# A gated block with cross-attention: channel order and transfers of the stacked score operands

## The chip, the cores and the metric

One core of a Trainium2 chip runs the kernel. The metric is the device time of one execution in microseconds; given are the median of three runs and one execution taken with the profiler.

## What is computed

The input x has 16 batches of 256 tokens with 256 channels, the context 16 batches of 256 tokens with 512 channels. Four steps add to x in turn, each behind a tanh gate: a depooled mix with a linear layer (part A below), three cycles of a small coupling network (part B), cross-attention from the normalised x to the context with 8 heads of 32 channels (part C), and a low-rank feed-forward layer (part D). The change lies in part C:

```
src_trans = ctx @ W_src.T + b_src          # 512 outputs: 256 for keys, 256 for values
tgt_trans = layernorm(x) @ W_tgt.T + b_tgt # 256 outputs: queries
(both times mask)
k, v, q   = 8 heads of 32 channels
scores    = q . k / sqrt(32), masked keys at -inf
attn      = softmax(scores)
x         = x + tanh(g) * (concat(layernorm(x), attn . v) @ W_out.T + b_out)
```

## The kernel before, in words

All engines have one program each, written out by hand, with semaphores between them; there is no planner. Only SP (SyncE) issues transfers, and all go through its one queue in the order of its program. Parts A and B are interleaved in twelve slots (`slot_b`); part C then runs over the 16 batches (`body_c`, `last_c`), part D over 8 groups of two batches. Engines other than SP use hardware loops for the middle batches of part C; SP's part is written out for all 16.

**Loads of part C.** `loads_c` (L426 to L436) lists eleven loads: the raw weights, the bias columns, the mask in three forms, and bias rows. SP issues them, with the seven of part D, in `weights_in` (L481) after batch 10 of part A. TensorE turns the raw weights (`turn_weights`, L1252) in slots 7 to 9 of part B into wsrcT, wtgtT and woutT.

**Keys and queries of a batch.** TensorE computes the keys of batch b+2 (`k_c`, L1374) and the queries of batch b+1 (`q_c`, L1401) while batch b is in its softmax. The result is transposed: 128 partitions are output channels, in two groups g of four heads each; head j of a group lies in partitions 32j to 32j+31, and the free dimension is the 256 tokens. VectorE adds the bias and masks (`biased`, L1898) into c_kT and c_qT.

**Parts.** The scores are computed in the fp32r format, with each operand split into a high and a low part. POOL (GpSimd) makes the keys' high and low part (`split_k`, L677 and L679), ScalarE the queries' high part (`high_q`, L938) and POOL their low part (`split_q`, L684). All four are in one tile, c_parts, with 128 partitions, for one batch at a time: the split of the next batch waits until the stacks of the batch before it have landed (semaphore c_stack_in).

**Stacks.** One product a head then covers three terms at once: the contraction has 97 rows, three strips of 32 (q high, q low, q high against k high, k high, k low) and one row with 1 against the mask. SP fills c_stack, one of two by turns, in `stack_c`: for each strip c and head j one copy (L526) of 32 partitions, queries and keys together, 128 KB; then the mask row (L530). That is 13 transfers a batch (STACK_DMAS). Before them SP waits for both key parts, for the queries' low part, and for the scores of two batches back, which read the same stack. Behind them SP issues the load of the context of batch b+2 (`stream_c`, L516). TensorE's `scores_c` (L1413) waits for all 13.

**Order on TensorE in `body_c`** (a batch b): scores of the first four heads; queries of b+1; values of b+1; transposes of the probabilities of b-1 (L1435); the output of b-1 (L1456); scores of the last four heads; transposes of the context of b+2 (L1366) and its keys (L1374); transposes of the normalised x of b+2 (L1384); the update (L1449). Before batch 0 TensorE prepares batches 0 and 1 and takes the last results of part B back (L1240), interleaved with the last slots of part B.

The names above are those of the rows: b_o, b_t, b_tt belong to part B; c_nmx is the negated maximum of the scores (VectorE, L1914), c_p the probabilities (ScalarE, L956), n_mv and n_tmp the statistics for part D.

Of the kernel before, what the change touches and what calls it, by code (L numbers as in the profile page):

```python
# [18 lines left out]
F32 = mybir.dt.float32  # L19
# [7 lines left out]
P = 128  # L27
B, S, D, DC = 16, 256, 256, 512
TILES = B * S // P
TS = S // P  # L30
DK = D // P
FK = DC // P
# [4 lines left out]
HEADS, HD = 8, 32  # L37
QH = 4
# [23 lines left out]
Q_LO, Q_HI, K_HI, K_LO = range(PARTS)  # L62
GCOL = 8
MASK_ROW = 3 * HD
STACK_DMAS = 3 * QH + 1
LEAD = 2
HEAD = 6
KB = 1024
# [48 lines left out]
def need(eng, sem, count):  # L117

    if isinstance(count, int) and count <= 0:
        return  # L120
    eng.wait_ge(sem, count)


def need_alone(eng, sem, count, passed):


    if isinstance(count, int):
        return need(eng, sem, count)
    eng.wait_ge(sem, count)
    eng.sem_inc(passed, 1)  # L130
# [33 lines left out]
def beyond(b, n):  # L164
    return isinstance(b, int) and b >= n
# [14 lines left out]
def build(nc, x, ctx_in, lens, mask, g_xattn, g_ffn, w_in, b_in, g_res, g_init,  # L180
# [7 lines left out]
    with ExitStack() as whole:  # L188
        def sb(name, shape, dt=F32, stack=whole):
            return stack.enter_context(nc.sbuf_tensor(name, shape, dt))  # L190

        def sem(name):
            return whole.enter_context(nc.semaphore(name))
# [26 lines left out]
        bk_col = sb("bk_col", [P, DK])  # L220
        bq_col = sb("bq_col", [P, DK])
# [90 lines left out]
        with ExitStack() as st:  # L312
            sb("raw_first", [P, 74 * KB // 4], F32, st)
            wsrc_raw = sb("wsrc_raw", [P, FK, DC], F32, st)
            wtgt_raw = sb("wtgt_raw", [P, DK, D], F32, st)
            wout_raw = sb("wout_raw", [P, DK, 2 * D], F32, st)
        with ExitStack() as st:
# [6 lines left out]
            c_stack = [None, sb("c_stack1", [MASK_ROW + 1, 2, QH, DK, S], F32R, st)]  # L324
# [9 lines left out]
            c_parts = sb("c_parts", [P, PARTS, DK, S], F32R, st)  # L334
# [5 lines left out]
        with ExitStack() as st:  # L340
# [24 lines left out]
        s_passed = sem("waits_passed")  # L365
# [26 lines left out]
        c_k_split, c_qhi_ok, c_qlo_ok, c_stack_in = (sem("c_" + n) for n in (  # L392
            "k_parts_ready", "q_high_ready", "q_low_ready", "stacks_in"))
        c_s_ps, c_mx_ok, c_p_ok, c_inv_ok, c_pn_ok = (sem("c_" + n) for n in (
            "scores_in_psum", "max_ready", "probs_ready", "inverse_sums_ready", "probs_normalised"))
# [15 lines left out]
        def column(v):  # L411
            return v.rearrange("(c p) -> p c", p=P)

        def row_on_all(v):
            return v.partition_broadcast(P)


        loads_a = [
            (gates_row[:, 0:4:2], g_xattn.rearrange("(o c) -> o c", o=1)),
# [3 lines left out]
        ]  # L423
        rows_a = [(ginit_b[:], row_on_all(g_init[0:D])), (bin_b[:], row_on_all(b_in))]
        loads_c = [
            (wsrc_raw[:], w_src.rearrange("(c p) f -> p c f", p=P)),  # L426
            (wtgt_raw[:], w_tgt.rearrange("(c p) f -> p c f", p=P)),
            (wout_raw[:], w_out.rearrange("(c p) f -> p c f", p=P)),
            (bk_col[:], column(b_src[0:D])), (bq_col[:], column(b_tgt)),
            (mask_b[:], mask.partition_broadcast(P)),  # L430
            (mask_col[:], mask.rearrange("b (k p) -> p b k", p=P)), (neg_row[:], mask),
            (bout_b[:], row_on_all(b_out)), (b2_b[:], row_on_all(b2)), (bv_b[:], row_on_all(b_src[D:2 * D])),
# [43 lines left out]
        def _(sp):  # L476
# [37 lines left out]
            def stream_c(b, s):  # L514
                need(sp, c_ctxT_ps, 2 * (b - 1))
                sp.dma_start(c_ctx[s][:], ctx_dram[b]).then_inc(c_ctx_in[s], 16)  # L516

            def stack_c(b, s):
                if isinstance(b, int) and b == 1:
                    sp.wait_ge(b_ok[3], 2 * PAIRS)  # L520
                need_alone(sp, c_k_split, 2 * b + 2, s_passed)
                need_alone(sp, c_qlo_ok, b + 1, s_passed)
                need_alone(sp, c_s_ps, 2 * TS * (b - 1), s_passed)
                for c, (first, step) in enumerate(((Q_HI, K_HI - Q_HI), (Q_LO, K_HI - Q_LO), (Q_HI, K_LO - Q_HI))):
                    for j in range(QH):
                        sp.dma_start(  # L526
                            c_stack[s][c * HD:(c + 1) * HD, :, j, :, :].rearrange("p a g t -> p a (g t)").bitcast(F32),
                            c_parts[j * HD:(j + 1) * HD, first:first + step + 1:step, :, :]
                            .rearrange("p a g t -> p a (g t)").bitcast(F32)).then_inc(c_stack_in, 16)
                sp.dma_start(  # L530
                    c_stack[s][MASK_ROW:MASK_ROW + 1, 1, :, :, :].rearrange("p j g t -> p (j g) t").bitcast(F32),
                    neg_row[b:b + 1, :].unsqueeze(1).to_broadcast([1, QH * DK, S])).then_inc(c_stack_in, 16)

            def body_stack(b, s):
                stack_c(b, s)
                if not beyond(b + 2, B):
                    stream_c(b + 2, s)

            stream_c(0, 0)
            stream_c(1, 1)  # L540
            sp.wait_ge(s_neg, 1)
            for b in range(B):
                body_stack(b, b % 2)

            def store(n, s):
                need(sp, d_y_ok, 2 * (n + 1))
# [16 lines left out]
        def _(pool):  # L563
# [110 lines left out]
            def split_k(b):  # L674
                need_alone(pool, c_k_ok, b + 1, s_passed)
                need_alone(pool, c_stack_in, 16 * STACK_DMAS * b, s_passed)
                nc.gpsimd.tensor_copy(c_parts[:, K_HI, :, :], c_kT[:]).then_inc(c_k_split, 1)  # L677
# [55 lines left out]
        def _(act):  # L733
# [201 lines left out]
            def high_q(b):  # L935
                need(act, c_q_ok, b + 1)
                need(act, c_stack_in, 16 * STACK_DMAS * b)
                nc.scalar.copy(c_parts[:, Q_HI, :, :], c_qT[:]).then_inc(c_qhi_ok, 1)  # L938
# [138 lines left out]
        def _(pe):  # L1077
# [327 lines left out]
            def scores_c(b, s, hg):  # L1405
                need(pe, c_stack_in, 16 * STACK_DMAS * (b + 1))
                if isinstance(b, int) and b < 2:
# [693 lines left out]
```

## Time and profile before

| what | us |
|---|---|
| median of three runs | 712.64 |
| lowest and highest of them | 712.11 and 713.82 |
| the profiled execution | 712.77 |
| its span, from first to last instruction | 710.7 |
| TensorE busy in it | 681.4 |
| VectorE busy | 512.4 |
| ScalarE busy | 418.1 |
| POOL busy | 209.7 |

The profiled execution has 2.07 us more than its span. Times in rows are microseconds from the start of the span. PE is TensorE's products, PEld its weight loads (they overlap), DVE VectorE, ACT ScalarE, POOL GpSimd, SPq the queue of SP. An L with a number is a line of the kernel.

### The profile page before, as it was taken

To read this page: it belongs to the slowest core of one execution; us is meant where nothing else is said; L and a number is where in the kernel's file an instruction comes from. 1 tells how busy PE (TensorE), PEld (TensorE's weight loads), DVE (VectorE), ACT (ScalarE), POOL (GpSimd) and SP (SyncE) were. 2 spreads that over 40 slices of the span, in tenths; PEclk is the share of its full clock that TensorE was granted. 3 is DMA by queue.
4 is the path that set the end of the run, shared out by engine and by line. 5 is a ranking of instruction groups with operands and counts; after the bars stand their busy time and mean duration, and the time that the engine had idled before them with its cause. 6 is when DMAs were issued, how large, how long until landed. Compare 5 with 4: busy or idle time off the path is not lost.

```text
span 710.7 us, 12199 instructions
## 1 busy us (share of the span) xinstructions
PE 681.4 (96%) x3877; PEld 478.4 (67%) x3877; DVE 512.4 (72%) x976; ACT 418.1 (59%) x1128; POOL 209.7 (30%) x285
## 2 busy tenths in 40 slices
PE   5799899999999999999999999999999998999997
PEld 3565555554544358788888888888888886756654
DVE  7864757776775458898889888888888888734422
ACT  7656665535555535656756657657667657645453
POOL 6564424200110033233343432332323330052110
PEclk9999999999999999999999999999999999999999
DMA  8721108401000004444323444333444323001012
GB/s 260 237 101 60 59 31 253 79 6 56 1 0 1 0 1 119 120 120 119 76 79 88 119 120 100 87 76 94 119 119 92 85 47 74 3 0 60 30 60 89
DMA packets 44970, 57.54 MB, mean 81 GB/s; under 512 B 13018, under 2 KB 23420, under 8 KB 44796
## 3 DMA queue, kind: packets, MB, share of 16 engines
q1 hardware_dynamic: 44924, 56.96, 29.8%
q8 instruction: 24, 0.39, 0.2%
q14 instruction: 22, 0.18, 0.1%
HBM read 27.46 MB, written 4.19 MB: 45 GB/s over the span
## 4 chain that ended last, share of the span: by engine, by line
PE 79%; ACT 7%; DVE 6%; issue 3%; POOL 2%; SPq 1%; DMA 1%; DVEq 0%; ACTq 0%; POOLq 0%
PE bank L1160 11%; PE bank L1456 8%; PE bank L1374 7%; PE bank L1435 7%; PE bank L1172 5%; PE bank L1392 5%; ACT c_p L956 5%; PE bank L1413 4%; PE bank L1449 4%; PE bank L1592 4%; PE bank L1136 3%; PE bank L1582 2%; PE bank L1140 2%; PE bank L1583 2%; DVE c_nmx L1914 2%
## 5 line engine op out<-in xcount | busy, mean ns | idle before, releaser
L956 ACT ACTIVATE c_p<-bank,c_nmx 128x256 f32<-128x256 f32 x256 | 117.3, 487 | 26.2 <-DVE c_nmx L1914 26.2
L1160 PE MATMUL bank<-b_o,cw 128*128 128x512 f32 x192 | 90.8, 603 | 0.2 <-ACT b_o L808 0.2
L1927 DVE TENSOR_TENSOR c_p<-c_p,c_inv 128x1024 f32<-128x1024 f32 x64 | 90.1, 1408 | 1.1
L1914 DVE TENSOR_REDUCE c_nmx<-bank 128x4 f32<-128x1024 f32 x64 | 75.4, 1218 | 13.4 <-PE bank L1413 13.4
L1435 PE MATMUL bank<-ident,c_p 128*128 128x128 f32 x512 | 65.4, 276 | 2.2 <-ACT c_p L956 1.6
L1435 PEld LDWEIGHTS bank<-ident,c_p 128*128 128x128 f32 x512 | 58.2, 142 | 10.0 <-issue 4.5
L784 ACT ACTIVATE b_h<-bank,cb 128x512 f32<-128x512 f32 x48 | 32.8, 686 | 51.2 <-PE bank L1160 51.2
L1059 ACT ACTIVATE d_h<-bank,b_col 128x512 f32<-128x512 f32 x64 | 39.6, 686 | 39.6 <-PE bank L1583 39.6
L1374 PE MATMUL bank<-c_ctxT,wsrcT 128*128 128x256 f32 x256 | 61.4, 385 | 0.7 <-ACT c_ctxT L932 0.7
L1160 PEld LDWEIGHTS bank<-b_o,cw 128*128 128x128 f32 x192 | 34.1, 190 | 41.3 <-issue 39.2
L1934 DVE COPY c_pT<-bank 128x512 f32<-128x512 f32 x64 | 43.7, 685 | 18.0 <-PE bank L1435 18.0
L1392 PE MATMUL bank<-wsrcT,c_ctxT 128*128 128x256 f32 x240 | 56.7, 379 | 0.0
L956 ACT ACTIVATION_READ_ACCUMULATOR c_p<-bank,c_nmx 128x1 f32 x256 | 56.3, 220 | 0.0
L684 POOL TENSOR_TENSOR c_parts<-c_qT,c_parts 128x512 fp32r<-128x512 f32 x16 | 20.9, 1303 | 118.4 <-ACT c_parts L938 118.4
L1374 PEld LDWEIGHTS bank<-c_ctxT,wsrcT 128*128 128x128 f32 x256 | 47.9, 192 | 7.0 <-ACT c_ctxT L932 0.9
L1392 PEld LDWEIGHTS bank<-wsrcT,c_ctxT 128*128 128x128 f32 x240 | 45.5, 190 | 6.2
L966 ACT COPY c_pT<-bank 128x512 f32<-128x512 f32 x64 | 38.0, 598 | 10.1 <-PE bank L1435 10.0
L1772 DVE TENSOR_SCALAR b_tt<-b_tt,k_tt,b_kb 128x256 f32<-128x256 f32 x48 | 19.7, 452 | 33.4 <-ACT b_tt L800 33.4
L1172 PE MATMUL bank<-b_h,cw 128*128 128x512 f32 x96 | 43.7, 593 | 0.0
L1413 PEld LDWEIGHTS bank<-c_stack 97*128 97x128 f32 x256 | 32.4, 189 | 13.0 <-issue 12.5
L971 ACT COPY c_upT<-bank 128x256 f32<-128x256 f32 x32 | 12.0, 375 | 46.9 <-PE bank L1449 46.9
L1413 PE MATMUL bank<-c_stack 97*128 97x256 f32 x256 | 38.9, 294 | 0.6 <-DMA c_stack<-neg_row 0.3
(194 smaller groups left out, 1384.4 us busy)
## 6 DMA issues: line engine op xcount, KB each, us to landing
c_stack<-c_parts SPq DMA_DIRECT2D x192, 128.0 KB
a_ctx<-in_ctx SPq DMA_DIRECT2D x16, 512.0 KB, 3.8
c_ctx<-in_ctx SPq DMA_DIRECT2D x16, 512.0 KB, 3.5
out_x<-x_sb SPq DMA_DIRECT2D x7, 512.0 KB, 2.9
x_sb<-in_x SPq DMA_DIRECT2D x3, 1024.0 KB, 10.2
mask_b<-in_mask_BxS_fk SPq DMA_DIRECT2D x1, 2048.0 KB, 12.1
x_sb<-in_x SPq DMA_DIRECT2D x2, 512.0 KB, 5.9
wsrc_raw<-in_L_xattn_W_src SPq DMA_DIRECT2D x1, 1024.0 KB, 6.8
```

The costliest lines, as they stand in the source:

```text
L956: op = nc.scalar.activation(c_p[hg][:, tc, j, :], scores(tc)[:, j, :], ACT.Exp, bias=c_nmx[hg][:, tc, j:j + 1], accum_out=c_sum[hg][:, tc, ...
L1059: op = nc.scalar.activation(d_h[j % 2][:, e, :], bank[2 * (j % 2) + e][:], ACT.Gelu_apprx_tanh, bias=b1_col[:, 2 * j + e:2 * j + e + 1])
L1160: op = mm(bank[2 * u + h][:], cw1[:, c, h * P:(h + 1) * P], b_o[n % LANES][:, c, :], start=c == 0, stop=c == DK - 1)
L1172: op = mm(bank[4 + u][:], cw2[:, c, :], b_h1[u][:, c, :], start=i == 0, stop=i == DK - 1)
L1374: op = mm(bank[dst][:, m * S:(m + 1) * S], wsrcT[:, f, m * P:(m + 1) * P], c_ctxT[s][:, f, :], start=f == 0, stop=f == FK - 1)
L1392: op = mm(bank[4][:, k * D:(k + 1) * D], c_ctxT[s][:, f, k * P:(k + 1) * P], wsrcT[:, f, D:2 * D], start=f == 0, stop=f == FK - 1)
L1413: op = mm(scores(tc)[:, j, :], c_stack[s][:, 0, j, hg, tc * P:(tc + 1) * P], c_stack[s][:, 1, j, hg, :], start=True, stop=True)
L1435: op = nc.tensor.transpose(bank[turned_bank(n, j)][:, q * S + tc * P:q * S + (tc + 1) * P], c_p[hg][:, tc, j, q * P:(q + 1) * P], ident[:])
L1456: return mm(bank[7][:, k * D:(k + 1) * D], src[:, k * P:(k + 1) * P], woutT[:, f, :], start=f == 0, stop=f == 2 * DK - 1)
L1914: v.tensor_reduce(c_nmx[hg][:, tc, :], scores(tc), AXIS.X, ALU.max, negate=True)\
L1927: v.tensor_tensor(pr, pr, c_inv[hg][:, :, js].unsqueeze(3).to_broadcast([P, TS, 2, S]), ALU.mult)\
L1934: v.tensor_copy(c_pT[hg][:, j, :], bank[turned_bank(n, j)][:]).then_inc(c_pT_dve, 1)
```

## The change

The key and query channels within each group of four heads are stored in the order (channel of the head, head), so that the four heads lie side by side: partition 4d + j in place of 32j + d. This is done by the loads of the weights' rows and of the biases; the values' rows keep their order. One copy then takes all 128 partitions of one part into one strip of the stack: six copies of 256 KB, three for the keys' side and three for the queries'. SP issues the keys' side, with the mask row, as soon as the keys' parts are ready, and the queries' side behind its own wait.

```diff
--- before.py
+++ after.py
@@ -62,7 +62,7 @@
 Q_LO, Q_HI, K_HI, K_LO = range(PARTS)
 GCOL = 8
 MASK_ROW = 3 * HD
-STACK_DMAS = 3 * QH + 1
+STACK_DMAS = 7
 LEAD = 2
 HEAD = 6
 KB = 1024
@@ -414,6 +414,9 @@
         def row_on_all(v):
             return v.partition_broadcast(P)
 
+        def heads_mixed(v):
+            return v.rearrange("(j d) o -> d j o", d=HD)
+
 
         loads_a = [
             (gates_row[:, 0:4:2], g_xattn.rearrange("(o c) -> o c", o=1)),
@@ -423,10 +426,14 @@
         ]
         rows_a = [(ginit_b[:], row_on_all(g_init[0:D])), (bin_b[:], row_on_all(b_in))]
         loads_c = [
-            (wsrc_raw[:], w_src.rearrange("(c p) f -> p c f", p=P)),
-            (wtgt_raw[:], w_tgt.rearrange("(c p) f -> p c f", p=P)),
+            *((wsrc_raw[:, c, :], heads_mixed(w_src[c * P:(c + 1) * P])) for c in range(DK)),
+            (wsrc_raw[:, DK:FK, :], w_src[D:2 * D].rearrange("(c p) f -> p c f", p=P)),
+            *((wtgt_raw[:, c, :], heads_mixed(w_tgt[c * P:(c + 1) * P])) for c in range(DK)),
             (wout_raw[:], w_out.rearrange("(c p) f -> p c f", p=P)),
-            (bk_col[:], column(b_src[0:D])), (bq_col[:], column(b_tgt)),
+            *((bk_col[:, c:c + 1], heads_mixed(b_src[c * P:(c + 1) * P].rearrange("(p o) -> p o", o=1)))
+              for c in range(DK)),
+            *((bq_col[:, c:c + 1], heads_mixed(b_tgt[c * P:(c + 1) * P].rearrange("(p o) -> p o", o=1)))
+              for c in range(DK)),
             (mask_b[:], mask.partition_broadcast(P)),
             (mask_col[:], mask.rearrange("b (k p) -> p b k", p=P)), (neg_row[:], mask),
             (bout_b[:], row_on_all(b_out)), (b2_b[:], row_on_all(b2)), (bv_b[:], row_on_all(b_src[D:2 * D])),
@@ -515,32 +522,34 @@
                 need(sp, c_ctxT_ps, 2 * (b - 1))
                 sp.dma_start(c_ctx[s][:], ctx_dram[b]).then_inc(c_ctx_in[s], 16)
 
-            def stack_c(b, s):
-                if isinstance(b, int) and b == 1:
+            def sides_c(b, s, side, firsts):
+                for c, part in enumerate(firsts):
+                    sp.dma_start(
+                        c_stack[s][c * HD:(c + 1) * HD, side, :, :, :].rearrange("p j g t -> p j (g t)").bitcast(F32),
+                        c_parts[:, part, :, :].rearrange("p g t -> p (g t)").bitcast(F32)).then_inc(c_stack_in, 16)
+
+            def keys_c(b, s):
+                if b == 1:
                     sp.wait_ge(b_ok[3], 2 * PAIRS)
-                need_alone(sp, c_k_split, 2 * b + 2, s_passed)
-                need_alone(sp, c_qlo_ok, b + 1, s_passed)
-                need_alone(sp, c_s_ps, 2 * TS * (b - 1), s_passed)
-                for c, (first, step) in enumerate(((Q_HI, K_HI - Q_HI), (Q_LO, K_HI - Q_LO), (Q_HI, K_LO - Q_HI))):
-                    for j in range(QH):
-                        sp.dma_start(
-                            c_stack[s][c * HD:(c + 1) * HD, :, j, :, :].rearrange("p a g t -> p a (g t)").bitcast(F32),
-                            c_parts[j * HD:(j + 1) * HD, first:first + step + 1:step, :, :]
-                            .rearrange("p a g t -> p a (g t)").bitcast(F32)).then_inc(c_stack_in, 16)
+                need(sp, c_k_split, 2 * b + 2)
+                need(sp, c_s_ps, 2 * TS * (b - 1))
+                sides_c(b, s, 1, (K_HI, K_HI, K_LO))
                 sp.dma_start(
                     c_stack[s][MASK_ROW:MASK_ROW + 1, 1, :, :, :].rearrange("p j g t -> p (j g) t").bitcast(F32),
                     neg_row[b:b + 1, :].unsqueeze(1).to_broadcast([1, QH * DK, S])).then_inc(c_stack_in, 16)
 
-            def body_stack(b, s):
-                stack_c(b, s)
-                if not beyond(b + 2, B):
-                    stream_c(b + 2, s)
+            def queries_c(b, s):
+                need(sp, c_qlo_ok, b + 1)
+                sides_c(b, s, 0, (Q_HI, Q_LO, Q_HI))
 
             stream_c(0, 0)
             stream_c(1, 1)
             sp.wait_ge(s_neg, 1)
             for b in range(B):
-                body_stack(b, b % 2)
+                keys_c(b, b % 2)
+                queries_c(b, b % 2)
+                if b + 2 < B:
+                    stream_c(b + 2, b % 2)
 
             def store(n, s):
                 need(sp, d_y_ok, 2 * (n + 1))
```

## Rows read from the trace of the kernel before

**Rows 1.** Waits, whole run: engine, line, releaser: us in total, times, longest

```profile
PE bank L1413 <- DMA c_stack<-neg_row: 0.3, 1, 0.3
...
PE bank L1366 <- DVE c_vb L1906: 0.9, 1, 0.9
PE bank L1374 <- ACT c_ctxT L932: 0.7, 1, 0.7
...
POOL c_parts L677 <- DVE c_kT L1898: 70.6, 15, 10.2
```

**Rows 2.** Steady batch: length, busy PE, PEld, DVE, ACT, POOL, clock, DMA share, GB/s

```profile
338.50:359.90 21.40, 21.38 (x153) 17.96 (x149) 19.18 (x35) 13.88 (x45) 7.74 (x10) 1.00 0.40 100
```

**Rows 3.** The chain of waits at batch 0: start, us, what

```profile
264.83 1.28 POOL c_parts L679
...
266.20 0.73 SPq L526
...
274.04 2.03 DMA c_stack<-neg_row
```

**Rows 4.** TensorE in order of time before batch 0: start, us, line, tiles, count, idle before

```profile
271.83 3.72 PE L1374 MATMUL bank<-c_ctxT,wsrcT 128*128 128x256 f32 x16
275.38 0.60 PE L1384 MATMUL bank<-ident,c_xn 128*128 128x128 f32 x4
276.31 1.18 PE L1413 MATMUL bank<-c_stack 97*128 97x256 f32 x8 [0.33 <-DMA c_stack<-neg_row]
```

**Rows 5.** Busy time by stretch while stack 0 moves (columns of rows 2)

```profile
266.00:267.50 1.50, 1.50 (x9) 0.89 (x6) 1.50 (x4) 0.89 (x2) 1.34 (x2) 1.00 0.00 0
...
268.50:275.00 6.50, 6.50 (x39) 5.79 (x39) 6.39 (x12) 1.88 (x4) 0.00 (x0) 1.00 0.88 205
```

**Rows 6.** SP's queue in order of time, stack of batch 1

```profile
284.08 9.28 SPq L526 DMA_DIRECT2D c_stack<-c_parts  x12
...
286.68 2.19 SPq L526 DMA_DIRECT2D c_stack<-c_parts  x1
...
293.40 0.72 SPq L530 DMA_DIRECT2D c_stack<-neg_row  x1
```

**Rows 7.** POOL, TensorE and SP in order of time, batch 1 and a steady batch

```profile
277.48 1.27 POOL L679 TENSOR_TENSOR c_parts<-c_kT,c_parts 128x512 fp32r<-128x512 f32 x1
...
282.72 1.27 POOL L684 TENSOR_TENSOR c_parts<-c_qT,c_parts 128x512 fp32r<-128x512 f32 x1 [2.12 <-ACT c_parts L938]
...
295.65 1.21 PE L1413 MATMUL bank<-c_stack 97*128 97x256 f32 x8
...
346.33 1.27 POOL L684 TENSOR_TENSOR c_parts<-c_qT,c_parts 128x512 fp32r<-128x512 f32 x1 [3.85 <-ACT c_parts L938]
...
347.66 7.68 SPq L526 DMA_DIRECT2D c_stack<-c_parts  x12
355.38 0.70 SPq L530 DMA_DIRECT2D c_stack<-neg_row  x1
...
359.89 1.22 PE L1413 MATMUL bank<-c_stack 97*128 97x256 f32 x8
```

**Rows 8.** SP and TensorE in order of time, stack and scores of the last batch

```profile
591.37 0.71 SPq L530 DMA_DIRECT2D c_stack<-neg_row  x1
...
594.39 1.22 PE L1413 MATMUL bank<-c_stack 97*128 97x256 f32 x8
```

**Rows 9.** SP and TensorE in order of time, loads of weights and first use

```profile
111.89 1.04 SPq L481 DMA_DIRECT2D bq_col<-in_L_xattn_b_tgt  x1
...
129.71 3.06 SPq L481 DMA_DIRECT2D v_sb<-in_L_ffn_V  x2
...
199.54 1.04 PE L1252 MATMUL bank<-ident,wsrc_raw 128*128 128x128 f32 x8
```

**Rows 10.** ScalarE in order of time, first exponential of batch 0

```profile
278.32 0.47 ACT L956 ACTIVATE c_p<-bank,c_nmx 128x256 f32<-128x256 f32 x1 [0.41 <-DVE c_nmx L1914]
```

**Rows 11.** Busy time by stretch after batch 0's idle times (columns of rows 2)

```profile
288.00:291.00 3.00, 3.00 (x11) 2.43 (x10) 1.72 (x3) 3.00 (x14) 0.00 (x0) 0.50 0.46 107
```

## The prediction

> **What bounds the kernel now.** The page names TensorE as the busiest engine, so I read its waits first, then the seam where the attention part (part C) begins, then one steady batch and the last one. The list of waits says what ended TensorE's idle time: in all its rows only one wait, of 0.3 us, ended with a stack transfer; the two larger ones of part C, 0.9 and 0.7 us, ended with VectorE's and ScalarE's work [rows 1]. In a steady batch TensorE works 21.38 of 21.40 us at a granted clock of 1.00 (its 2.4 GHz level), while VectorE works 19.18 us and the DMA engines have a share of 0.40 [rows 2]. So part C runs at the pace of TensorE, and a transfer matters only where it lands later than TensorE's earlier work ends.
>
> The place where it does is batch 0. SP waits for the low part of the keys (POOL, 264.83 + 1.28 us), issues twelve copies from 266.20 to 274.04 us, 0.65 us each, and then the mask row, which lands 2.03 us later, at 276.07 [rows 3]. TensorE ends the preparation of batch 1 at 275.38 + 0.60 = 275.98 us and starts the scores at 276.31, after 0.33 us of idle time [rows 4]. The chain of waits passes through SP there, which looks like eight microseconds of transfer on the path; but TensorE has other work beside all of it up to 275.98 us, without idle time [rows 4]. From this seam I take the whole gain, 0.33 us and not the length of the chain.
>
> **The change, part by part.**
>
> *Copies of the stacks.* Twelve copies of 128 KB go and six of 256 KB come: the same 1.57 MB a batch, and in both forms one contiguous run is 2 KB. Issues fall from 13 to 7. At 0.65 us each that is 4.6 us in place of 8.5 us [rows 3]. No row shows a copy from 128 partitions into 32, so its data rate has to be bounded. The fast end: issue was the limit, and the engines, at a share of 0.88 with 205 GB/s [rows 5], could give 205 / 0.88 = 233 GB/s; 1.57 MB is then 6.7 us. The middle: 205 GB/s stays, 7.7 us. The slow end: batch 1, whose copies began at 284.08 and whose mask row, issued at 293.40, landed some 2.03 us later, near 295.4 [rows 3, 6]: 1.57 MB in 11.3 us, 139 GB/s. I take 205 GB/s: it is the rate of the same bytes in runs of the same length, steady over 6.5 us. Data began 1.3 us after the first issue (nothing moves before 267.5) [rows 5]. So the last byte arrives at 267.5 + 7.7 = 275.2. From there to the landing it takes nothing at the least and at the most what the same sum leaves of before, 276.07 - 275.2 = 0.9 us; I take the middle, 0.4, thus 275.6 us, ahead of 275.98. The fast end gives 274.6; 0.9 us in place of 0.4 gives 276.1, the first rival below.
>
> A rule of the Trainium skill speaks against the change here: "SBUF — State Buffer", section "Door 1: The DMA port swizzle (why [64,N] ≈ [32,N])", says that the rate of a transfer depends on how many of 16 ports its partitions reach, that 32 partitions reach eight, and gives 27.2 GB/s for each. By it the writes, still into strips of 32 partitions, stay below about 218 GB/s though the reads now span 128, so that wider copies buy no rate; the sum would have 7.2 us of data and the same end.
>
> *Order and waits.* SP now waits for the keys' parts and for the scores of two batches back, issues three copies and the mask row, then waits for the low part of the queries and issues three more. In batch 0 POOL made the queries' part before the keys' parts, so both waits end at 266.12 us and the order brings nothing. In batch 1 the keys' parts are ready at 277.48 + 1.27 = 278.75 us and the queries at 282.72 + 1.27 = 283.99 [rows 7]; the keys' side lands before the queries are there, and three copies remain: half the data at the slow 139 GB/s is 5.7 us, plus 1.3 and 0.4, landing near 291.4, for scores that start at 295.65 [rows 7]. Before, the landing at about 295.4 left only 0.2 us there; it becomes over 4. In a steady batch SP issues the mask row at 355.38, which lands near 357.4, for scores at 359.89 [rows 7]. With the queries ready at 346.33 + 1.27 = 347.60 and three copies to go, the landing moves to about 353 and the slack of 2.5 us to about 7: worth nothing, costs nothing. The last batch is the same: mask row at 591.37, landing near 593.4, scores at 594.39 [rows 8].
> Behind SP's new waits stand the queries' copies and the load of the context of two batches on. Six issues less stand ahead of that load, so it goes out some 3.9 us earlier than now. Behind the landing of all seven transfers stand POOL's split of the next keys and ScalarE's high part of the queries; but POOL's 70.6 us of waiting before its key split all end with VectorE's keys, none with a transfer [rows 1], so an earlier landing frees nobody.
>
> *Weights and biases in mixed order.* Eleven loads become sixteen: five more issues on SP, at up to 1.04 us each some 5 us at most, with the same bytes, in runs of 1 or 2 KB for the weights and 4 bytes for the biases. SP's last load is issued by 129.71 + 3.06 = 132.8 us; the first turn of a weight on TensorE is at 199.54 us [rows 9]. The cover is TensorE's 67 us of part B; without it they would cost their 5 us. Cost: nothing. TensorE, ScalarE and VectorE run the same instructions on the same shapes everywhere, at no cost.
>
> *Sum.* The profiled execution took 712.77 us: its span of 710.7 and 2.07 around it. TensorE's wait of 0.33 us goes. What is late next is the softmax of batch 0: the first exponential waited 0.41 us for VectorE's maxima, after ScalarE had been free [rows 10], and the maxima need these scores; so all of it can follow 0.33 us earlier. 712.77 - 0.33 = 712.44. The median of the runs lies 0.13 us under the profiled execution, so I forecast **712.3 us**.
>
> **The rivals.** I take 0.3% (2.1 us) as about what a measurement of this kernel can tell from no change: faster begins at 710.5, slower at 714.8.
>
> *No gain at all.* If the data rate and not the issue set the end, or if the wide copies are a little slower than 205 GB/s, or take the 0.9 us to land, batch 0 lands at 276.1 as before and the time stays 712.6. For it: 205 GB/s is just 128 KB per 0.64 us, so the rows of batch 0 can't tell rate from issue. Against it: in a steady batch too the twelve issues took an even 7.68 us [rows 7]; a queue held back by data would be less even. 0.25.
>
> *Slower: batch 0 waits for slow copies.* Each copy now reads 128 partitions and writes 32, a form that no row shows. At the 139 GB/s of batch 1 its data ends at 267.5 + 11.3 = 278.8 us and lands at 279.2: 279.2 - 275.98 = 3.2 us of waiting in place of 0.33, so 712.6 + 2.9 = 715.5 us. It decides from 2.1 us of added wait on, a landing at 278.4, a rate under 1.57 MB / (278.4 - 0.4 - 267.5) = 150 GB/s. Only batch 0 pays; all others have the slack above. Against it: what stretched batch 1 was one issue of 2.19 us in the midst of normal ones [rows 6], not the rate of the copies. 0.07.
>
> *The clock.* After TensorE's idle times of 0.9 and 0.7 us [rows 1] at the end of batch 0, the granted clock was 0.50 (1.2 GHz) from 288 to 291 us [rows 11], with TensorE busy throughout: 3 us of work that takes 1.5 us at 2.4 GHz. These idle times wait for VectorE and ScalarE and not for a stack, so they stay; but all of it comes 0.33 us earlier, and the fall may turn on that. If it doesn't come: 712.3 - 1.5 = 710.8. If another of its size comes elsewhere: 713.8. 0.06 and 0.04.
>
> *The change does not do what it says.* The order of the channels could force runs shorter than 2 KB and so more of them. The patterns say otherwise: the last dimension of both sides stays 512 numbers. It would end as the slower rival does, and is in its chance.
>
> **How the numbers follow.** Forecast 0.58, no gain 0.25, slow copies 0.07, clock kept 0.06, clock lost twice 0.04. The first two hold 0.83, at 712.3 and 712.6; the runs before lay 0.5 us below and 1.2 us above their median, which makes 711.8 to 713.8. To take in part of the kept clock I go down to 711.4. Faster (under 710.5) takes half of the kept clock's chance with its run-to-run spread: 0.04. Slower takes most of the slow copies and the top of the clock lost twice: 0.07. The rest, 0.89, is the same.
>
> **What would show it.** In the profile after: no idle time before the scores of batch 0 that ends with a transfer, these scores at 275.98; the last of seven issues at about 270.1 us; in each steady batch two groups on SP, four issues near its start and three after the queries; still 21.40 us a batch. If the landing in batch 0 stays near 276.1, the rate set it and not the issue. The prediction is wrong if the period of the batches moves, if TensorE waits over 1 us for a stack anywhere, or if a time under 711 comes without a change of the clock.

## The result, and the profile after

The changed kernel is slower: a median of 719.80 us over four executions (717.20 to 720.99) against 712.61 us for the kernel before (four executions). The medians lie 7.2 us apart, 1.0%; the means lie 6.7 us apart, and the ratio follows them: 1.0093 with a 95% interval of 1.0063 to 1.0124. The profiled execution was the lowest of the four, 717.20 us, with a span of 715.4 us. One of the four executions of e5_gaps below fell in a slow state (995.34 us at a granted clock of 0.66) and is left out of its figures.

The number of issues came out as intended, and the order too. SP's queue in order of time, in batches 0 and 1:

```profile
264.27 1.98 SPq L527 DMA_DIRECT2D c_stack<-c_parts  x3
266.29 0.75 SPq L537 DMA_DIRECT2D c_stack<-neg_row  x1
267.08 1.89 SPq L527 DMA_DIRECT2D c_stack<-c_parts  x3
269.01 0.61 SPq L523 DMA_DIRECT2D c_ctx<-in_ctx  x1
281.33 1.85 SPq L527 DMA_DIRECT2D c_stack<-c_parts  x3
```

Seven issues take 4.7 us (264.27 to 268.97), where thirteen took 8.5 [rows 3]. But TensorE, in order of time:

```profile
273.46 0.60 PE L1393 MATMUL bank<-ident,c_xn 128*128 128x128 f32 x4
279.40 2.04 PE L1422 MATMUL bank<-c_stack 97*128 97x256 f32 x8 [5.34 <-DMA c_stack<-c_parts]
281.24 3.62 PE L1410 MATMUL bank<-c_xnTq,wtgtT 128*128 128x256 f32 x8
284.65 2.02 PE L1401 MATMUL bank<-wsrcT,c_ctxT 128*128 128x256 f32 x8
```

It was ready at 274.06 us and waited 5.34 us for the stack, where it had waited 0.33 [rows 4]. The copies were all issued by then; it is their data that took the time. Busy time by stretch (the columns of rows 2; the last two are the DMA share and GB/s):

```profile
264.00:265.50 1.50, 1.50 (x8) 0.84 (x5) 1.50 (x4) 0.82 (x2) 1.43 (x2) 1.00 0.00 0
...
268.00:270.00 2.00, 2.00 (x19) 1.83 (x17) 2.00 (x5) 1.23 (x3) 0.00 (x0) 1.00 1.07 122
270.00:272.00 2.00, 2.00 (x11) 1.77 (x11) 1.93 (x4) 0.65 (x2) 0.00 (x0) 1.00 1.08 123
272.00:274.00 2.00, 2.00 (x12) 1.59 (x10) 2.00 (x5) 0.00 (x0) 0.00 (x0) 1.00 1.11 127
274.00:276.00 2.00, 0.06 (x1) 0.00 (x0) 0.80 (x3) 1.87 (x2) 0.00 (x0) 1.00 1.04 119
```

122 GB/s at a DMA share of 1.07, where the copies before moved 205 GB/s at 0.88 [rows 5]. A share of 1 is not a rate: the engines were held longer for the same bytes. During the wait the granted clock fell:

```profile
274.00:279.40 5.40, 0.06 (x1) 0.03 (x1) 0.80 (x3) 1.87 (x2) 0.12 (x1) 0.88 1.03 147
279.40:284.00 4.60, 4.60 (x15) 4.06 (x16) 2.36 (x2) 2.11 (x9) 3.57 (x3) 0.50 0.43 99
284.00:285.00 1.00, 1.00 (x5) 0.79 (x4) 0.10 (x1) 1.00 (x6) 0.00 (x0) 0.55 1.10 127
...
321.70:343.10 21.40, 21.38 (x152) 17.98 (x148) 19.19 (x35) 13.88 (x45) 7.75 (x10) 1.00 0.62 99
```

From 279.4 us on TensorE worked for some 5.5 us at 0.50 (1.2 GHz): all of the 4.6 us up to 284.0, and nine tenths of the microsecond after them. The last line is a steady batch: 21.38 us busy of 21.40, as before [rows 2]; only the DMA share rose, from 0.40 to 0.62 for the same bytes.

The books of the profiled pair need the later starts of the same work, first before, then after:

```profile
280.79 1.04 PE L1240 MATMUL bank<-ident,b_o 128*128 128x128 f32 x8
287.14 3.01 PE L1374 MATMUL bank<-c_ctxT,wsrcT 128*128 128x256 f32 x8 [0.69 <-ACT c_ctxT L932]
292.39 1.89 PE L1374 MATMUL bank<-c_ctxT,wsrcT 128*128 128x256 f32 x8
```

```profile
286.50 1.04 PE L1249 MATMUL bank<-ident,b_o 128*128 128x128 f32 x8
292.42 1.99 PE L1383 MATMUL bank<-c_ctxT,wsrcT 128*128 128x256 f32 x8 [0.69 <-ACT c_ctxT L941]
296.17 1.06 PE L1444 MATMUL bank<-ident,c_p 128*128 128x128 f32 x8 [0.76 <-ACT c_p L965]
297.07 1.89 PE L1383 MATMUL bank<-c_ctxT,wsrcT 128*128 128x256 f32 x8
```

| term | us |
|---|---|
| TensorE ready for the first scores at 274.06 in place of 275.98 | -1.9 |
| wait for stack 0, 5.34 in place of 0.33 | +5.0 |
| slow clock behind it: 279.40 to 286.50 took 7.1, 276.31 to 280.79 took 4.5 | +2.6 |
| shorter wait for c_vb, 0.45 in place of 0.88 | -0.4 |
| the slow stretch of before [rows 11] did not occur, less a new wait | -0.6 |

The sum is 4.7 us, the whole difference of the spans (715.4 and 710.7). The slow stretch had lasted over 3 us, but its absence gave only 0.6 us (292.42 to 297.07 against 287.14 to 292.39), because TensorE then caught up with ScalarE and waited 0.76 us for the probabilities.

The first term is luck of this execution, as far as the runs show. In the profiled executions of the other five kernels with the mixed loads TensorE was ready between 274.4 and 275.5 us, and in four with the loads of before (before, e6_forms, e9_held, e10_forms2) between 274.0 and 276.0; the two ranges overlap. The other three executions of the changed kernel took 719.6 to 721.0 us.

### The profile page after: what moved, and what is told of

Its sections match the earlier page's. It is cut to its first block, busy times and chain, and to the rows that moved or that the text cites. A ratio compares the mean times of both kernels' runs of the same rounds, so it can differ in the third digit from the quotient of the medians.

```text
span 715.4 us, 12108 instructions
## 1 busy us (share of the span) xinstructions
PE 680.8 (95%) x3877; PEld 478.0 (67%) x3877; DVE 512.2 (72%) x976; ACT 418.2 (58%) x1128; POOL 208.7 (29%) x285
## 4 chain that ended last, share of the span: by engine, by line
PE 78%; ACT 8%; DVE 6%; issue 3%; POOL 2%; DMA 2%; SPq 1%; DVEq 0%; ACTq 0%; POOLq 0%
PE bank L1169 11%; PE bank L1465 8%; PE bank L1444 7%; PE bank L1383 7%; ACT c_p L965 5%; PE bank L1181 5%; PE bank L1401 5%; PE bank L1422 4%; PE bank L1458 4%; PE bank L1601 4%; PE bank L1145 3%; PE bank L1591 2%; PE bank L1149 2%; PE bank L1592 2%; DVE c_nmx L1923 2%
## 5 line engine op out<-in xcount | busy, mean ns | idle before, releaser
L1444 PE MATMUL bank<-ident,c_p 128*128 128x128 f32 x512 | 64.9, 274 | 2.9 <-ACT c_p L965 2.3
L1444 PEld LDWEIGHTS bank<-ident,c_p 128*128 128x128 f32 x512 | 57.3, 141 | 11.0 <-issue 5.6
```

Source lines behind the costliest of these rows:

```text
L1444: op = nc.tensor.transpose(bank[turned_bank(n, j)][:, q * S + tc * P:q * S + (tc + 1) * P], c_p[hg][:, tc, j, q * P:(q + 1) * P], ident[:])
```

## The experiments

**Where in the kernel is the loss?** Three kernels ask this. In `e4_first12` batch 0 alone goes back to twelve copies, one for each head and strip (in the mixed order these read every fourth partition); the others stay as changed.

```diff
             for b in range(B):
-                keys_c(b, b % 2)
-                queries_c(b, b % 2)
+                if b == 0:
+                    strided_c(b, b % 2)
+                else:
+                    keys_c(b, b % 2)
+                    queries_c(b, b % 2)
...
+                for c, (first, step) in enumerate(...):
+                    for j in range(QH):
+                        sp.dma_start(c_stack[s][c * HD:(c + 1) * HD, :, j, :, :]...,
+                                     c_parts[j:P:QH, first:first + step + 1:step, :, :]...)
```

The counts of landed copies that the other engines wait for follow; that part is left out here.

> The changed kernel with the stack of batch 0 alone filled by the twelve copies of one head each; batches 1 to 15 keep six wide copies and early keys. Theory 1 (only batch 0 pays): 712 to 713.5 us, TensorE's wait for a stack under 0.5 us, the granted clock at 0.50 in one stretch of 3 us at most after it. Rival (the slow copies cost something in every batch, through contention or through the context load behind them): 715 us or more, with a period of the batches over 21.5 us or new waits of 0.2 us and more.

Measured: 715.44 us, ratio to before 1.0049 (1.0031 to 1.0068). The wait was 3.22 us, not under 0.5: these copies are slow too, at some 150 GB/s.

```profile
278.01 1.22 PE L1446 MATMUL bank<-c_stack 97*128 97x256 f32 x8 [3.22 <-DMA c_stack<-neg_row]
279.03 3.57 PE L1434 MATMUL bank<-c_xnTq,wtgtT 128*128 128x256 f32 x8
```

So both numbers that I gave missed, and the time is even past the rival's 715 us; but neither sign of the rival is there. A batch takes 21.40 us still, and no other wait is for a stack. In the profiled pair there are 2.9 us more of waiting and 1.7 us for the clock, which fell 1 us after the wait and stayed at 0.50 for some 3.3 us; TensorE was ready 1.2 us earlier, and 0.4 and 0.6 us came off as in the changed kernel. That makes 2.4 of the 2.5 us between the spans, all of it in batch 0.

In `e7_queries_first` all copies stay wide; in batch 0 alone the queries' side, which POOL makes first, is issued first.

```diff
-                keys_c(b, b % 2)
+                if b > 0:
+                    keys_c(b, b % 2)
                 queries_c(b, b % 2)
+                if b == 0:
+                    keys_c(b, b % 2)
```

> The changed kernel, but in batch 0 alone the queries' three copies go ahead of the keys' side, since POOL has their parts 3.9 us earlier. Theory 1 (the loss is the late landing in batch 0 and the clock that follows): the first data moves from some 261.5 us on, 1.57 MB at 122 GB/s end at 274.5 and land at 274.9, TensorE is ready at 274.0: a wait of about 0.9 us in place of 5.3, no long stretch of slow clock right after it, and a time of 712.5 to 714 us. Rival (wide copies cost in all batches): 715 us or more.

Measured: 712.69 us over ten executions, ratio 1.0008 (0.9996 to 1.0020). TensorE in order of time:

```profile
274.71 0.60 PE L1396 MATMUL bank<-ident,c_xn 128*128 128x128 f32 x4
276.70 1.19 PE L1425 MATMUL bank<-c_stack 97*128 97x256 f32 x8 [1.40 <-DMA c_stack<-neg_row]
277.73 1.89 PE L1413 MATMUL bank<-c_xnTq,wtgtT 128*128 128x256 f32 x8
```

The wait is 1.40 us, more than the 0.9 I had estimated, and the product after it takes 1.89 us, the time at 2.4 GHz, where it took 3.62. Fifteen wide stacks, the early keys and the mixed loads together cost nothing that the medians of ten and nineteen executions show, and nothing near 7 us.

One reservation stands against "nothing". Nine of the ten executions had a mean granted clock of 0.997 or 0.998, and spans of 710.1 to 711.4 us. The kernel of before had that clock in seven of nineteen, with spans of 708.7 to 709.2; in the other twelve, at 0.993 to 0.995, they were 710.0 to 712.6. At a like clock e7_queries_first is thus some 2 us longer. Its wait, 1.1 us longer than before's, is about half of that; what the other half is (the slow copies of later batches, the loads, or something else) no run shows.

`e9_held` is the opposite: the kernel of before, with fast copies everywhere, where only the last four copies and the mask row of batch 0 are held back.

```diff
                     for j in range(QH):
+                        if b == 0 and c * QH + j == 3 * QH - 4:
+                            sp.wait_ge(c_xnT_ps, 2)
                         sp.dma_start(
```

> The kernel of before with its fast copies, but the last four copies and the mask row of batch 0 are held back until TensorE has ended its work ahead of the scores (275.98 us), so that the stack lands some 5.3 us after that (five issues of 0.65 us and 2.03 us), as late as in the changed kernel; no other batch is touched. Theory 1 (a late landing in batch 0 and the slow clock after it are the whole loss): 718.5 to 720.5 us, with 1.2 GHz for some 6 us after the wait. Rival (part of the loss comes from the slow copies of the other batches): 717.5 us or less, and the rest up to 719.8 is theirs.

Measured: 718.52 us, ratio 1.0093 (1.0074 to 1.0111), the ratio of the change itself. The wait came to 4.86 us, and the clock fell as in the changed kernel, for a shorter time:

```profile
274.99 0.60 PE L1386 MATMUL bank<-ident,c_xn 128*128 128x128 f32 x4
280.44 2.05 PE L1415 MATMUL bank<-c_stack 97*128 97x256 f32 x8 [4.86 <-DMA c_stack<-neg_row]
282.29 2.62 PE L1403 MATMUL bank<-c_xnTq,wtgtT 128*128 128x256 f32 x8
```

The same kernel, busy time and clock in the stretch behind the wait:

```profile
280.40:284.00 3.60, 3.56 (x13) 3.30 (x14) 2.33 (x2) 1.07 (x5) 3.46 (x3) 0.53 0.33 124
```

A late landing in batch 0 and the clock behind it, put into the old kernel by hand, give 6.4 us over the 712.13 us of before in that comparison. The wait was 0.5 us shorter than the change's, and the slow clock behind it cost 1.5 us (280.44 to 286.46 for the 4.5 us of before) where it had cost 2.6, because it lasted some 3.3 us and not 5.5 (nor the 6 expected); against this, the later slow stretch of before came here too. The interval is 1.3 us wide on either side, so a loss of about 1 us in the other batches is not excluded by this run.

**Did the early keys matter?** `e1_late` keeps the wide copies and undoes the order.

```diff
                 need(sp, c_k_split, 2 * b + 2)
+                need(sp, c_qlo_ok, b + 1)
                 need(sp, c_s_ps, 2 * TS * (b - 1))
```

> The changed kernel with its early keys undone: SP waits for the queries' low part too before it issues any of the seven transfers; the form of the copies stays. Theory 1 (the wide copies themselves move only some 122 GB/s, so stack 0 lands 5 us too late for TensorE and everything else is hidden): nothing changes against the changed kernel, TensorE waits 5 to 5.5 us for stack 0 and a time of 717 to 721 us, since both waits end together in batch 0; in a steady batch the landing moves from about 6 us ahead of the scores to 0 or 1 us ahead (1.57 MB at 122 GB/s is 12.9 us, started 12.2 us before the scores), so a small wait per batch is possible, up to 2 us each, 740 us at the worst. Theory 2 (the early issue costs, because keys' copies stand in the queue when context loads or queries should go): faster than the changed kernel, 712 to 714 us.

Measured: 791.02 us, ratio 1.1098 (1.1036 to 1.1160), far beyond both. The list of waits (engine, line, releaser: us in total, times, longest us):

```profile
POOL c_parts L687 <- DMA c_stack<-c_parts: 104.0, 15, 14.3
...
PE bank L1423 <- DMA c_stack<-c_parts: 49.0, 16, 5.4
```

And busy time in one stretch of the same kernel, late in part C:

```profile
426.40:450.80 24.40, 23.34 (x136) 20.06 (x140) 16.04 (x24) 13.12 (x44) 9.82 (x9) 0.86 0.49 69
```

POOL waits because it may split the next keys only after the stack has landed. TensorE waited in all sixteen batches, some 2.9 us each after the first. In the four batches after batch 0 (304 to 402 us) the clock still stayed at 1.00, with waits of 2.5 to 2.9 us; then it was 0.93 over one stretch of 24.4 us and 0.86 over each of the next four. TensorE was busy for 711.9 us in place of 680.8 with the same instructions. My bound counted the waits, with 2 us each, and forgot the clock. So the change has two halves of opposite sign: the wide copies alone would cost 11%, and the early keys take nearly all of that back. Their order in the queue costs nothing (the second theory falls).

**What makes the copies slow?** `e2_strided` undoes the width and keeps the mixed order, with twelve copies as in e4_first12 in all batches and the old waits.

```diff
-                keys_c(b, b % 2)
-                queries_c(b, b % 2)
+                strided_c(b, b % 2)
```

> Channel order as in the changed kernel, but the stacks filled by twelve copies again, each from the 32 partitions of one head (every fourth one), queries and keys together, with all waits first. Theory 1 in the form that the width of a copy (128 partitions read, strips of 8 KB written) is slow: the rate is back at 205 GB/s, stack 0 lands at 276 on the clock of the profile of before, TensorE waits under 0.5 us, the time is 712 to 713.5 us. In the form that the mixed order of partitions is slow to read whatever the copy: DMA share near 1 at some 122 GB/s, wait of 5 us, 717 to 721 us. Rival (the mixed order of the loads costs something in the earlier parts): 1.57 MB moves at 205 GB/s but the time stays over 715 us.

Measured: 729.16 us, ratio 1.0247 (1.0226 to 1.0268). The rate during stack 0 is between the two:

```profile
268.00:270.00 2.00, 2.00 (x18) 1.88 (x17) 2.00 (x5) 0.92 (x2) 0.00 (x0) 1.00 1.11 158
270.00:272.00 2.00, 2.00 (x12) 1.73 (x11) 1.93 (x5) 0.96 (x3) 0.00 (x0) 1.00 1.04 145
272.00:274.00 2.00, 2.00 (x12) 1.72 (x12) 2.00 (x4) 0.00 (x0) 0.00 (x0) 1.00 1.10 151
```

Neither answer I had offered fits: the width is not the whole of it, since the strided copies of 32 partitions, 128 KB each as before, give some 150 and not 205 GB/s. With all waits first they delay every batch (14.2 us of waits for stacks in sixteen batches).

`e5_gaps` takes the other suspect, the 8 KB that each partition of the stack receives in one piece: with queries and keys of a head side by side these are four runs of 2 KB with gaps. The mask row takes two transfers then (left out below).

```diff
-sb("c_stack1", [MASK_ROW + 1, 2, QH, DK, S], F32R, st)
+sb("c_stack1", [MASK_ROW + 1, QH, 2, DK, S], F32R, st)
...
-c_stack[s][c * HD:(c + 1) * HD, side, :, :, :]
+c_stack[s][c * HD:(c + 1) * HD, :, side, :, :]
```

> The changed kernel with another layout of the stack: queries and keys of one head side by side, so that one partition receives four runs of 2 KB with gaps of 2 KB between them, and not 8 KB in one piece; the mask row takes two transfers instead of one. Reads, number and size of the copies as in the changed kernel. Theory W (four runs of one partition in one piece, or packets of more than 2 KB, slow the writes): the rate goes back to about 205 GB/s, TensorE's wait under 0.5 us, 712 to 713.5 us. Theory R (what is slow is the reading of 128 neighbouring partitions, or engines that meet at one port): 122 GB/s as before, a wait of 5 to 6 us (one issue more), 717 to 721 us.

Measured: 719.02 us (three executions), ratio 1.0098 (1.0077 to 1.0120). TensorE waited 5.4 us, the rate was 118 to 128 GB/s. The runs are not the cause.

So two kernels measured forms of copies by themselves, in the kernel of before: after the stack of each of ten batches, four extra copies of 256 KB, one form for a batch, each waited for before the next is issued. They read the turned weights and write a part of the memory that is free then.

```diff
+            def probe(b):
+                sp.wait_ge(c_ctx_in[b % 2], 16 * ((b + 2) // 2 + 1))
+                for i in range(4):
+                    sp.dma_start(*forms[b - 3]).then_inc(s_probe, 16)
+                    sp.wait_ge(s_probe, 64 * (b - 3) + 16 * (i + 1))
```

> The kernel of before, with four extra copies of 256 KB after the stack of each of ten batches (3 to 12), one form for each batch, each copy waited for before the next; they read the turned weights and write into a part of the memory that is free then, so the result stays; the time has no meaning here, only the spacing of the issues and the GB/s of the DMA engines by form. The forms in order: (1) 128 partitions to the same 128, (2) 128 to 32, the form of the change, (3) 32 to 128, (4) 32 to the same 32 in runs of 8 KB, (5) the same in runs of 2000 bytes, (6) partitions 64 to 95 to 0 to 31, (7) every fourth partition to 0 to 31, (8) 0 to 31 to every fourth, (9) every fourth to the same, (10) 128 to 64 to 95. Theory A (engines meet at the partitions that a narrow side has, so a narrow write or a narrow read gives the limit): 1 fastest, 2, 3, 4 and 10 alike near 200 GB/s at most. Theory B (what counts is that each engine reads and writes the partitions of the same place; a copy whose two sides are laid out differently is slow): 1, 4, 5 and 9 fast (1 and 9 over 250, 4 and 5 some 200 GB/s), 2, 3, 10 near 122, 7 and 8 near 148 GB/s. Theory C (runs or size: 8 KB against 2 KB): 4 and 5 differ, and 2 is like 5.

> The kernel of before with extra copies of 256 KB as in e6_forms, other forms: (1) partitions 0 to 31 to the same, (2) 32 to 63 to 0 to 31, (3) 16 to 47 to 0 to 31, (4) 4 to 35 to 0 to 31, (5) 0 to 63 to the same, (6) 64 to 127 to 0 to 63, (7) every second of 128 to 0 to 63, (8) 0 to 63 to 0 to 31, (9) 128 to 0 to 63, (10) 128 to 0 to 31. The spacing of the issues counts; e6_forms gave 3.0 us for 32 to the same 32 and 4.0 us for 128 to 32. Theory B1 (each engine should read and write the same place; any shift of one side is slow): 3 and 4 take 3.5 us or more, 2 and 6 stay at 3.0 because they were as fast as their like in e6_forms (64 partitions apart). Theory B2 (a shift is harmless; slow is a copy whose two sides divide the partitions differently, so that engines meet at few partitions on one side): 2, 3, 4 and 6 all stay near 3.0, 7, 8 and 9 lie between 3.0 and 4.0 us, 10 at 4.0 us.

Each was profiled in one execution. The spacing from the second issue to the third, in us (the spacings within a form agree within 0.1 us, but for the first of the very first form and one of 3.72 where partitions 4 to 35 were read):

| from | to | e6_forms | e10_forms2 |
|---|---|---|---|
| 128 | the same 128 | 2.31 | |
| every fourth of 128 | the same | 2.37 | |
| 32 | the same 32, run of 8 KB | 3.05 | 2.99 |
| 32 | the same 32, runs of 2000 bytes | 3.02 | |
| 64 to 95 | 0 to 31 | 2.90 | |
| 32 to 63 | 0 to 31 | | 2.91 |
| 16 to 47 | 0 to 31 | | 2.93 |
| 4 to 35 | 0 to 31 | | 2.95 (last) |
| 64 | the same 64 | | 3.01 |
| 64 to 127 | 0 to 63 | | 2.90 |
| 0 to 31 | every fourth | 3.44 | |
| 32 | 128 | 3.54 | |
| every fourth | 0 to 31 | 3.85 | |
| every second | 0 to 63 | | 3.90 |
| 64 | 32 | | 3.91 |
| 128 | 64 | | 4.02 |
| 128 | 32 (the form of the change) | 4.00 | 4.00 |
| 128 | 64 to 95 | 4.00 | |

Three classes stand out. A copy to the same partitions, or to ones shifted by 4, 16, 32 or 64, takes 2.9 to 3.1 us where its sides are 32 or 64 neighbours, and 2.3 to 2.4 where they spread over all 128. A copy whose sides divide the partitions differently takes 3.4 to 4.0, and halving the number (128 to 64, 64 to 32) is as slow as quartering it: the second theory of e10_forms2 holds, with its "between 3.0 and 4.0" at the top of that range (3.90, 3.91, 4.02). The first theory of each (a narrow side, or any shift) falls, and so does the third of e6_forms, as runs of 8 KB and of 2000 bytes take the same (3.05 and 3.02).

How a slow copy goes is seen in quarters of a microsecond. First 128 partitions to the same, in e6_forms, the columns as before:

```profile
343.93:344.18 0.25, 0.25 (x5) 0.25 (x4) 0.22 (x3) 0.11 (x1) 0.00 (x0) 1.00 0.44 172
344.18:344.43 0.25, 0.25 (x5) 0.25 (x4) 0.25 (x1) 0.06 (x1) 0.00 (x0) 1.00 1.02 393
344.43:344.68 0.25, 0.25 (x5) 0.25 (x3) 0.25 (x1) 0.25 (x1) 0.00 (x0) 1.00 1.01 393
344.68:344.93 0.25, 0.25 (x3) 0.23 (x3) 0.25 (x1) 0.25 (x2) 0.00 (x0) 1.00 0.25 90
```

Then 128 to 32, the same 256 KB, in the same kernel:

```profile
364.83:365.08 0.25, 0.25 (x3) 0.02 (x1) 0.25 (x1) 0.25 (x3) 0.00 (x0) 1.00 0.89 352
365.08:365.33 0.25, 0.22 (x3) 0.24 (x3) 0.25 (x2) 0.25 (x1) 0.00 (x0) 1.00 1.15 377
365.33:365.58 0.25, 0.25 (x4) 0.25 (x3) 0.22 (x3) 0.12 (x1) 0.00 (x0) 1.00 1.28 139
365.58:365.83 0.25, 0.25 (x5) 0.25 (x4) 0.25 (x1) 0.05 (x1) 0.00 (x0) 1.00 1.04 106
365.83:366.08 0.25, 0.25 (x5) 0.25 (x4) 0.25 (x1) 0.25 (x1) 0.00 (x0) 1.00 0.55 66
```

It starts as fast as the other and falls to some 110 GB/s after half a microsecond, with every engine still held. That looks like data piling up ahead of a few places of the side written; which engine writes where is not in the trace, so this reading is an inference. It would also say why a single copy does not show the low rate from its start and a queue of them does.

**Was the small gain there at all?** In `e8_ones_later` the kernel of before starts its copies of batch 0 earlier, as POOL's fill of the row of ones (1.80 us) moves behind the key split.

```diff
             split_q(0)
-            ones_c(0, c_qlo_ok, 1)
             split_k(0)
+            ones_c(0, c_k_split, 2)
```

> The kernel of before, but POOL fills the row of ones of stack 0 (1.80 us) after it has split the keys of batch 0, and not ahead of it. The copies then start 1.8 us earlier. If the 0.33 us of TensorE's wait in batch 0 was all that the stacks cost before, the wait goes and the time falls by 0.3 us to 712.1, which can't be told from no change: 711.5 to 712.5 us.

Measured: median 711.55 us over ten executions, but the ratio is 1.0001 (0.9990 to 1.0011). TensorE's wait for the stack is gone from the list and a new one stands ahead of it:

```profile
269.79 1.04 PE L1366 MATMUL bank<-ident,c_ctx 128*128 128x128 f32 x8
271.59 1.09 PE L1240 MATMUL bank<-ident,b_o 128*128 128x128 f32 x8 [0.77 <-DVE b_o L1779]
272.52 3.62 PE L1374 MATMUL bank<-c_ctxT,wsrcT 128*128 128x256 f32 x16
...
276.33 1.20 PE L1413 MATMUL bank<-c_stack 97*128 97x256 f32 x8
```

The scores of batch 0 begin without a wait, at 276.33 us, the 276.31 of before. But the edit moved more than the copies. VectorE before, then VectorE and POOL in e8_ones_later:

```profile
267.33 0.74 DVE L1772 TENSOR_SCALAR b_tt<-b_tt,k_tt,b_kb 128x256 f32<-128x256 f32 x2
```

```profile
267.05 1.82 DVE L1772 TENSOR_SCALAR b_tt<-b_tt,k_tt,b_kb 128x256 f32<-128x256 f32 x2
267.13 1.27 POOL L671 TENSOR_TENSOR x_sb<-x_sb,bout_b 128x512 f32<-128x512 f32 x1
```

POOL's addition at L671, which comes after the fill in its program, ran at 266.07 us before and now runs beside two instructions of VectorE's update, which take 1.82 us in place of 0.74. TensorE, 0.27 us ahead of before at 269.79, then waits 0.77 us for that update. That the one delays the other is my reading of these rows; no run tests it. The copies also start only 0.9 us earlier (265.29 against 266.20), not 1.8, because POOL waits for VectorE's keys first. So this way of taking the wait away is worth nothing that can be measured; whether the 0.33 us could be had without the side effect stays open.

## Why the prediction was wrong, point by point

*What bounds the kernel.* Right: TensorE sets the pace, only batch 0 can wait for a stack, and a steady batch takes 21.40 us still.

*The count of issues.* Right: seven issues in 4.7 us, estimated at 4.6.

*The rate of the wide copy.* This is the step that failed: "I take 205 GB/s: it is the rate of the same bytes in runs of the same length". The rate measured is 122 GB/s. Bytes and run length were the wrong measure of likeness; what counts is whether both sides divide the partitions alike, and no copy in the trace of before did anything else. The slow end of my bounds, 139 GB/s, did not hold it either: it came from a stretch of batch 1 that one issue of 2.19 us had stretched, which says nothing on the rate of any copy. A form that no row shows has no lower bound in rows of another form. With 122 GB/s the same sum gives, on the clock of the profile after, data from 265.5 + 12.9 = 278.4 and a landing near 278.8; TensorE got it by 279.40.

*The rule of the Trainium skill* that I weighed, in "SBUF — State Buffer", section "Door 1: The DMA port swizzle (why [64,N] ≈ [32,N])", spoke against the gain, but not enough: it allows 218 GB/s for writes to 32 partitions, and 122 were measured. Where both sides are alike it agrees with the forms: 64 neighbours took 3.01 us as 32 did (2.99 to 3.05), and 32 partitions spread over all 128 took 2.37 us, near the 2.31 of all 128. Counting the partitions of one side was not sufficient: a copy of 32 partitions to the same 32 has the same narrow side and took 3.0 us, the form of the change 4.0.

*The rival "batch 0 waits for slow copies"* was the case that came, with the place I gave and the sign. It was priced at 715.5 us for 139 GB/s and had 0.07. Two of its terms were too small: the wait (3.2 us estimated, 5.34 measured) and the clock, which I had treated as a rival by itself instead of as a part of this one. [Rows 11] showed that 1.6 us of idle time in the same batch was followed by 1.2 GHz; a wait of over 3 us had to be priced with such a stretch as well. 712.6 + 5.0 + 2.6 = 720.2 us, against 719.8 measured.

*Order and waits.* "Worth nothing, costs nothing" was right for fast copies and wrong for these. In the steady batch the queries' copies are issued at 352.29 us:

```profile
345.86 1.86 SPq L527 DMA_DIRECT2D c_stack<-c_parts  x3
...
352.29 1.88 SPq L527 DMA_DIRECT2D c_stack<-c_parts  x3
...
364.55 1.21 PE L1422 MATMUL bank<-c_stack 97*128 97x256 f32 x8
```

Half the data at 122 GB/s is 6.4 us, so I estimate the landing at 352.3 + 1.3 + 6.4 + 0.4 = 360.4 us, 4 us ahead of the scores. With the whole stack behind the queries it would be 366.9, late by more than 2 us: e1_late showed 2.9 us a batch.

*The loads in mixed order* cost nothing that can be told apart: e7_queries_first has them, with the reservation made there. *The gain of 0.33 us* is neither confirmed nor refuted: e8_ones_later removed that wait, but its side effect put another one in its place.

*The clock as a rival.* In the profile after, the slow stretch at 288 us was gone, and that was worth 0.6 us and not the 1.5 of the sum. The prediction had passed over a wait of TensorE in part C that is in the same list: 1.6 us in three waits for ScalarE's probabilities (L1435). It grew to 2.3 us in four (L1444) once the clock was kept. The chance of 0.06 was small too: of the nineteen executions of before that were taken later, seven had a clock of 0.997 or 0.998.

*The chances.* 0.07 for the slow copies was too little for a quantity I had just called unbounded by any row, when its error costs ten times what the forecast gains (2.9 us against 0.33). With 0.3 us to win and all of the landing at risk in batch 0, the side on which an error falls should have set the chances.

## What to carry to other kernels

Fewer transfers are not faster transfers: a copy within the on-chip memory whose two sides divide the partitions differently (128 to 32, every fourth to neighbours) ran at some 120 and 150 GB/s in a queue here, one of 32 partitions to 32 neighbours at 205, so measure the form of a copy by itself before the layout of a kernel is built on it. Before a stage whose operands need a pipeline of transfers, look at its first pass: in fifteen batches the slack hid the slow copies, and only because the keys' side went out early; the first batch, with no slack, paid. And price a TensorE wait with the slow clock that may follow it: here 5.0 us more of waiting brought 2.6 us of slow clock with it.

## What the runs showed of the hardware that I had not expected

A copy of 256 KB from 128 partitions to 64 is as slow as one to 32 (4.02 and 4.00 us, against 2.31 to the same 128), while a shift by 4, 16, 32 or 64 partitions costs nothing (2.9 us each, against 3.0 for the same partitions). A slow copy begins at up to 377 GB/s and falls to 106. The reverse direction, 32 to 128, is less slow, 3.54 us.

In e1_late waits of 2.5 to 2.9 us left the granted clock of TensorE at 1.00 for four batches; later ones, of 2.5 to 4.5 us, went with a clock of 0.86 over a batch, and the busy time rose from 680.8 to 711.9 us. After a single idle time of 1.40 us in e7_queries_first the clock stayed at 1.00 for the next 14 us; after one of 3.22 us in e4_first12 it fell 1 us later, for some 3.3 us; after one of 4.86 us in e9_held TensorE resumed at 0.50, also for some 3.3 us.

Two instructions of VectorE that take 0.74 us together took 1.82 us in e8_ones_later, where an addition on POOL ran beside them.

What stays open: how the sixteen engines share a copy whose sides differ, and thus why halving is as slow as quartering; whether the copies could be given a faster form in the mixed order; what makes e7_queries_first some 2 us longer than before at a like clock; and whether TensorE's readiness 1.9 us earlier in the profiled execution has a cause in the change.
